# Attention output of a gated layer on one TensorE: rows from score weights instead of columns from value weights

## Chip, cores and metric

The kernel runs on one core of a Trainium2 chip. The metric is the device time of one execution in microseconds (us).

## What is computed

The layer has two parts. The first is a gated long convolution over heads (`_L0_xattn_ref`), the second a routed linear attention (`_L0_ffn_ref`). The change touches only the end of the second part. Cut to that, the reference is:

```python
qk = einsum('bhld,bhmd->bhlm', q_exp, k_exp) * HDK ** (-0.5)
qk = qk * tril(ones)                      # causal mask, no softmax
o = einsum('bhlm,bhmd->bhld', qk, v)      # 16 heads, v is 32 wide in each
mu, var = mean(o, -1), var(o, -1)         # of each head's 32 values
o = (o - mu) / sqrt(var + EPS)
out = (silu(g) * o.reshape(b, l, d)) @ Wout
x = x + tanh(g_ffn) * out
```

All of it is in float32. The mean over a head is taken out of `Wv` during setup, so `o` has mean zero and its variance is the mean of its squares.

## The kernel before

A step handles one slice of the batch and head axes: a tile of 128 rows by 512 columns. There are 32 slices (`NH`) and 35 steps, h from -2 to 32, written out one after another. A step works on four slices at different stages: `pre` makes the products and the normalised query of slice h+2 and h+3, `front` convolves slice h+1, `back` projects and scores slice h, and `tail` finishes slice h-1 (attention output, norm, gate, output projection). So the attention output runs in 32 steps, h = 1 to 32. In steps 31 and 32 there is no convolution left beside it.

Each engine has a program of its own, in an order fixed by hand, and the engines meet at semaphores. Nothing is planned at run time. What follows is the order on each engine around the change.

TensorE (L353 to L438): four transposes of z, convolutions 0 and 1 (`conv`, 3 and 6 matmuls of 512 columns), then `attention_output` (L325), then convolution 2 (9 matmuls), then four transposes of `oT` back into rows (L373), then `conv_last` (12 matmuls of 256 to 64 columns, L301), then the projections for q, k and the logits (L386 to L391, 24 matmuls), convolution 3, the count matmul (L398), the transposes of qn, the projection for v (L407), and further work, to the scores (L348) at the end of the step. `transpose4` is the helper of L265; the convolution matmuls carry L289, the projections L315.

`attention_output` (L325 to L335) waits for the four masks and for v. It makes 16 matmuls, one for each head. The stationary operand is a head's 32 columns of `v_sb`, the moving operand the head's 128 x 128 masked scores `att`. The output is 32 partitions by 128 columns, so four heads lie side by side in four column groups of the array. The result is the transpose of o. ScalarE copies it out of bank 4 into `oT` (L508), and TensorE transposes it back into bank 4 (L373).

ScalarE (L485 on): y_raw copies (L499), `kv_round` 0 (L483), copy of oT (L508), `kv_round` 1 (L483), the two Silu of y (L522, L524), Square of o (L529), then copies of q and k (L544, L547) and the query norm (L558, L562).

VectorE (L765 on): the multiply of convolution 0, y_conv (L773), the multiply of convolution 1, y low part (L784), statistics of x (L789 to L797), the multiply of convolution 2, the sum of squares (L803) and variance plus eps (L806), `multiply_last`, the router selection, then `gated` (L831, L836).

GpSimd (L641 on): products and low parts of kv 0 and 1 (L624 to L633), the power for the query norm (`rstd1`, L639 from L649), the power for the attention norm (`o_rstd`, L639 from L651), the rotation (L657 to L665), products 2 and 3, and the power for z.

SyncE issues all loads and stores of a step; the change does not touch it.

Of the kernel before, what the change touches and what calls it, by code (L numbers as in the profile page):

```python
# [13 lines left out]
P = 128  # L14
# [10 lines left out]
def can_wait(value):  # L25

    return not isinstance(value, int) or value > 0


def flamingo_gated_layer(nc, x, ctx_t, g_xattn, g_ffn, ssm_kernel, ssm_D, conv_w, Wq, Wk, Wv, Wg,  # L30
# [35 lines left out]
    with ExitStack() as stack:  # L66
        def sb(name, *free):
            return stack.enter_context(nc.sbuf_tensor(name, [P, *free], F32))
# [9 lines left out]
        def sem(name):  # L78
            return stack.enter_context(nc.semaphore(name))
# [65 lines left out]
        keT = sb("keT", CH, P)  # L145
        att = sb("att", CH, CH, P)
        o_sq = sb("o_sq", RH, HDV)
        oT = sb("oT", CH, P)
        gated = sb("gated", DV)
        out_sb = sb("out_sb", 2, L)  # L150
        yT_p = parts("yT", CH, P)
# [21 lines left out]
        gatedT_ps, zT_ps, out_ps, logit_ps, q_ps, v_ps, g_ps, cnt_ps = (  # L173
            sem(n) for n in ("gatedT_ps", "zT_ps", "out_ps", "logit_ps", "q_ps", "v_ps", "g_ps", "cnt_ps"))
        conv_ps = [sem(f"conv_ps{i}") for i in range(CH)]
        qeT_ps, keT_ps, qT_ps, xo_ps, oT_ps, o_ps = (
            sem(n) for n in ("qeT_ps", "keT_ps", "qT_ps", "xo_ps", "oT_ps", "o_ps"))
        attn_ps = [sem(f"attn_ps{i}") for i in range(CH)]

        gatedT_high, y_cur, y_ready, th_ready, qk_copied, v_copied, gate_ready = (  # L180
            sem(n) for n in ("gatedT_high", "y_cur", "y_ready", "th_ready", "qk_copied", "v_copied", "gate_ready"))
        qeT_sb, keT_sb, qx_ready, oT_sb, o_squared = (
            sem(n) for n in ("qeT_sb", "keT_sb", "qx_ready", "oT_sb", "o_squared"))
        y_high = sem("y_high")
        kv_high = [sem(f"kv_high{i}") for i in range(CH)]

# [75 lines left out]
        def _(eng):  # L262
            def transpose4(dst, src, last):
                for c in range(CH):
                    ins = nc.tensor.transpose(dst[:, c * P:(c + 1) * P], src(c), ident)  # L265
                ins.then_inc(last, 1)
# [55 lines left out]
            def step(t, p, q, tail, back, front, pre):  # L322
                h = 2 * t + p

                def attention_output():  # L325

                    for r in range(CH):
                        eng.wait_ge(mask_done[r], h)
                    eng.wait_ge(v_copied, h)
                    for c in range(CH):  # L330
                        for r in range(CH):
                            i = CH * c + r
                            ins = nc.tensor.matmul(bank[4][r * HDV:(r + 1) * HDV, c * P:(c + 1) * P],  # L333
                                                   v_sb[:, i * HDV:(i + 1) * HDV], att[:, r, c, :], start=True, stop=True)
                    ins.then_inc(oT_ps, 1)  # L335

                def scores():

# [29 lines left out]
                if front:  # L368
                    eng.wait_ge(mul_done[0], h + 2)
                    conv(p, 2, h + 1)  # L370
                if tail:
                    eng.wait_ge(oT_sb, h)
                    transpose4(bank[4], lambda c: oT[:, c, :], o_ps)  # L373
                if front:
                    if can_wait(h):
                        eng.wait_ge(mask_done[0], h)
# [66 lines left out]
        def _(eng):  # L443
# [41 lines left out]
            def step(t, p, q, tail, back, front, pre):  # L485
# [16 lines left out]
                if pre:  # L502
                    kv_round(p, 0, h + 2)
                if tail:
                    eng.wait_ge(oT_ps, h)
                    if can_wait(h - 1):
                        eng.wait_ge(o_ps, h - 1)
                    eng.activation(oT[:, :, :], bank[4][:, :].rearrange("p (c n) -> p c n", c=CH), ACT.Copy  # L508
                                   ).then_inc(oT_sb, 1)
                if pre:  # L510
                    kv_round(p, 1, h + 2)
                if first_step:
# [5 lines left out]
                if back:  # L518
# [3 lines left out]
                    eng.activation(yT_p[0][:, :, :], y_raw[:, :, :], ACT.Silu).then_inc(y_high, 1)  # L522
                    eng.wait_ge(y_high, h + 1)
                    eng.activation(y_raw[:, :, :], y_raw[:, :, :], ACT.Silu).then_inc(y_ready, 1)  # L524
                if tail:
                    eng.wait_ge(o_ps, h)
                    if can_wait(h - 1):
                        eng.wait_ge(o_summed, h - 1)
                    eng.activation(o_sq[:, :, :], bank[4][:, :].rearrange("p (a n) -> p a n", n=HDV), ACT.Square  # L529
                                   ).then_inc(o_squared, 1)  # L530
                if isinstance(h, int) and h == 0:
                    output_weights_high()
                if first_step:
# [35 lines left out]
                if back:  # L569
                    eng.wait_ge(v_ps, h + 1)  # L570
                    if can_wait(h):
                        eng.wait_ge(oT_ps, h)
                    eng.activation(v_sb[:, :], bank[4][:, :], ACT.Copy).then_inc(v_copied, 1)
                if tail:
                    eng.wait_ge(gatedT_ps, h)
# [33 lines left out]
        @block.gpsimd  # L609
        def _(eng):  # L610
            eng.memset(minus_half[:, :], -0.5).then_inc(half_ready, 1)
            eng.wait_ge(half_ready, 1)
            eng.wait_ge(s_consts, 16)

            def products(t, p, c, h2):

                if c == 0:
                    eng.wait_ge(s_kx[p], 16 * (t + 2))

                if c >= 2:  # L620
                    eng.wait_ge(kv_ready[c - 2], h2 + 1)
                elif can_wait(h2):
                    eng.wait_ge(kv_ready[c + 2], h2)
                eng.tensor_tensor(view(kv[:, c % 2, 0:FULL], [[ROW, NROT], [1, ROW]]),  # L624
                                  view(kx[:, p, c, 0:ROW], [[0, NROT], [1, ROW]]),
                                  view(kx[:, p, c, 0:ROW], [[NB, NROT], [1, ROW]]), ALU.mult)
                eng.tensor_tensor(kv[:, c % 2, FULL:FULL + HALF], kx[:, p, c, 0:HALF],  # L627
                                  kx[:, p, c, HALF:2 * HALF], ALU.mult).then_inc(kv_made[c], 1)

            def kv_rest(p, c, h2):  # L630

                eng.wait_ge(kv_high[c], h2 + 1)
                eng.tensor_tensor(kv_p[1][:, p, c, :], kv[:, c % 2, :], kv_p[0][:, p, c, :].bitcast(F32), ALU.subtract  # L633
                                  ).then_inc(kv_ready[c], 1)


            def rsqrt(dst, src, n, ready, value, done):
                eng.wait_ge(ready, value)
                eng.tensor_tensor(dst[:, 0:n], src[:, 0:n], minus_half[:, 0:n], ALU.pow).then_inc(done, 1)  # L639

            def step(t, p, q, tail, back, front, pre):  # L641
                h = 2 * t + p
                if pre:
                    products(t, p, 0, h + 2)
                    products(t, p, 1, h + 2)
                    kv_rest(p, 0, h + 2)
                    kv_rest(p, 1, h + 2)
                if pre:
                    rsqrt(rstd1, ve1, 1, ve1_ready, h + 3, rstd1_ready)  # L649
                if tail:  # L650
                    rsqrt(o_rstd, o_ve, RH, o_ve_ready, h, o_rstd_ready)  # L651
                if back:

                    eng.wait_ge(qk_copied, h + 1)
                    if can_wait(h):
                        eng.wait_ge(qke_ready, h)
                    eng.tensor_tensor(rot_a[:, :, :], qk_sb[:, :, :], view(const[:, C_COS:C_COS + 1], [[0, 2 * RH], [1, HDK]]),  # L657
                                      ALU.mult).then_inc(rot_prod, 1)
                    hf = HDK // 2
                    for a in range(2):  # L660
                        s = const[:, C_SIN + a * hf:C_SIN + a * hf + 1]
                        eng.tensor_tensor(rot_b[:, :, a * hf:(a + 1) * hf], qk_sb[:, :, (1 - a) * hf:(2 - a) * hf],  # L662
                                          view(s, [[0, 2 * RH], [1, hf]]), ALU.mult).then_inc(rot_prod, 1)
                    eng.wait_ge(rot_prod, 3 * h + 3)
                    eng.tensor_tensor(rot_a[:, :, :], rot_a[:, :, :], rot_b[:, :, :], ALU.add).then_inc(rot_ready, 1)  # L665
                if pre:
                    products(t, p, 2, h + 2)
                    products(t, p, 3, h + 2)
                    kv_rest(p, 2, h + 2)
                    kv_rest(p, 3, h + 2)  # L670
                if front:
                    rsqrt(rstd2, ve2, 1, ve2_ready, h + 2, rstd2_ready)

            run(eng, step)

        @block.vector
        def _(eng):
# [84 lines left out]
            def step(t, p, q, tail, back, front, pre):  # L762
# [12 lines left out]
                    ins.then_inc(y_conv, 1)  # L775
                if front:
                    multiply(p, 1, h + 1)
                if setup_step:
                    weights_low(1)
                if back:  # L780
# [16 lines left out]
                    eng.tensor_scalar(ve1[:, :], mv1[:, 1:2], EPS, None, ALU.add).then_inc(ve1_ready, 1)  # L797
                if front:
                    multiply(p, 2, h + 1)
                if tail:  # L800

                    eng.wait_ge(o_squared, h)
                    eng.tensor_reduce(o_var[:, :], o_sq[:, :, :], AX_X, ALU.add).then_inc(o_summed, 1)  # L803
                    eng.wait_ge(o_summed, h)
                    eng.wait_ge(eps_ready, h)
                    eng.scalar_tensor_tensor(out=o_ve[:, :], in0=o_var[:, :], scalar=1.0 / HDV, in1=eps_w[:, :],  # L806
                                             op0=ALU.mult, op1=ALU.add).then_inc(o_ve_ready, 1)
                if front:
                    multiply_last(p, h + 1)
                if back:  # L810
# [75 lines left out]
                if back:  # L886
                    for r in range(CH):
                        eng.wait_ge(attn_ps[r], h + 1)
                        if r == 0 and can_wait(h):
                            eng.wait_ge(oT_ps, h)  # L890
                        mask_scores(r)

            run(eng, step)
# [47 lines left out]
```

## Time and profile before

| what | value |
|---|---|
| median of 3 runs | 985.41 us (985.02 to 985.78) |
| profiled execution, its own time | 986.2 us |
| its span | 984.4 us |
| TensorE clock granted, mean | 0.982 of full |
| TensorE matmul busy | 923.5 us, 94% |
| TensorE weight load busy | 792.4 us, 81% |
| VectorE, GpSimd, ScalarE busy | 624.8, 673.0, 426.9 us |

Busy time of TensorE is modelled and matmuls overlap, so 94% does not say that every cycle is used. It says that nearly no time passes without a matmul under way. Weight loads (PEld) are listed apart and run beside the matmuls. A float32 matmul that is not a transpose shows as two records of PE and two of PEld, so 16 matmuls show as 32.

### The profile page before, as it was taken

What the parts mean: (1) busy time and instruction counts of PE and PEld (TensorE: products, weight loads), DVE (VectorE), ACT (ScalarE), POOL (GpSimd) and SP (SyncE); (2) the same over time, 40 slices, a digit from 0 to 9 for tenths busy, and PEclk for the clock granted to TensorE, in tenths of its full rate; (3) what the DMA queues carried; (4) which work ended last, traced back from release to release, by engine and by line L of the source; (5) the groups of instructions that cost most, each with busy time, mean ns of one, the idle gap of its engine ahead of it and who ended that gap; (6) DMA issues with size and microseconds to landing.
All of it is one profiled execution on the core that took longest, in us unless ns stands there. A gap on an engine that the chain in (4) does not pass through costs nothing.

```text
span 984.4 us, 18833 instructions
## 1 busy us (share of the span) xinstructions
PE 923.5 (94%) x7168; PEld 792.4 (81%) x7168; DVE 624.8 (63%) x1400; ACT 426.9 (43%) x906; POOL 673.0 (68%) x613
## 2 busy tenths in 40 slices
PE   1598999999999999999999999999999999999973
PEld 1487888888888888888888888888888888888862
DVE  4765666667666666766666676666666766666542
ACT  2464444444444444444444444444444444454320
POOL 6676668776666777766677776667777666686321
PEclk9899999999999999999999999999999999999996
DMA  8111221012222201222220122222112222210000
GB/s 278 50 46 47 60 60 49 17 55 60 61 59 60 57 21 43 60 61 60 60 60 21 39 60 61 59 61 59 36 28 58 60 61 60 60 41 11 5 11 21
DMA packets 25992, 52.50 MB, mean 53 GB/s; under 512 B 2544, under 2 KB 3696, under 8 KB 25904
## 3 DMA queue, kind: packets, MB, share of 16 engines
q1 hardware_dynamic: 22304, 46.59, 17.5%
q10 hardware_dynamic: 3600, 4.72, 1.5%
q8 instruction: 57, 0.93, 0.4%
q14 instruction: 31, 0.25, 0.1%
HBM read 42.75 MB, written 8.55 MB: 52 GB/s over the span
## 4 chain that ended last, share of the span: by engine, by line
PE 81%; DMA 5%; issue 5%; POOL 4%; DVE 3%; ACT 1%; SPq 0%; POOLq 0%; ACTq 0%
PE bank L315 33%; PE bank L289 19%; PE bank L276 11%; PE bank L265 8%; DMA x_in<-in_x 4%; PE bank L301 4%; PE bank L348 3%; PE bank L333 3%; POOL o_rstd L639 2%; DMA w_all<-in_L_ffn_Wv 1%; POOL rstd L639 1%; POOL rot_b L662 1%; POOL kv_low L633 0%; DVE gated L831 0%; DVE out_sb L884 0%
## 5 line engine op out<-in xcount | busy, mean ns | idle before, releaser
L633 POOL TENSOR_TENSOR kv_low<-kv,kv_high 128x576 fp32r<-128x576 f32 x128 | 182.1, 1435 | 136.8 <-ACT kv_high L483 136.8
L289 PE MATMUL bank<-kv_high,toep 128*128 128x512 f32 x640 | 225.2, 409 | 11.0 <-DVE z_terms L736 5.6
L624 POOL TENSOR_TENSOR kv<-kx 128x512 f32<-128x512 f32 x128 | 159.5, 1246 | 6.6 <-DMA const<-shape_consts 6.6
L289 PEld LDWEIGHTS bank<-kv_high,toep 128*128 128x128 f32 x640 | 122.5, 191 | 42.3 <-DVE z_terms L736 11.5
L639 POOL TENSOR_TENSOR o_rstd<-o_ve,minus_half 128x16 f32<-128x16 f32 x32 | 93.1, 2910 | 79.8 <-DVE o_ve L806 79.8
L289 PE MATMUL bank<-kv_low,toep 128*128 128x512 f32 x320 | 126.8, 396 | 0.0
L483 ACT ACTIVATE kv_high<-kv 128x576 fp32r<-128x576 f32 x128 | 87.7, 688 | 87.6 <-POOL kv L627 87.6
L315 PE MATMUL bank<-w_all_high,yT_high 128*128 128x512 f32 (+2 forms) x512 | 119.7, 355 | 3.0 <-DVE gated L831 3.0
L276 PE MATMUL bank<-const,z_terms 128*128 128x128 f32 x1024 | 117.1, 273 | 1.0 <-ACT qx L472 1.0
L276 PEld LDWEIGHTS bank<-const,z_terms 128*128 128x128 f32 x1024 | 112.8, 140 | 1.3 <-ACT qx L472 1.2
L315 PE MATMUL bank<-w_all_low,yT_high 128*128 128x512 f32 (+2 forms) x512 | 112.5, 341 | 0.0
L315 PE MATMUL bank<-w_all_high,yT_low 128*128 128x512 f32 (+2 forms) x512 | 106.7, 341 | 0.0
L884 DVE TENSOR_TENSOR out_sb<-bank,x 128x512 f32<-128x512 f32 x32 | 22.1, 692 | 125.6 <-PE bank L315 125.6
L746 DVE TENSOR_TENSOR qke<-rot_a,sel 128x1024 f32<-128x1024 f32 x32 | 69.1, 2160 | 38.9 <-POOL rot_a L665 38.9
L315 PEld LDWEIGHTS bank<-w_all_low,yT_high 128*128 128x128 f32 x512 | 83.8, 189 | 11.2
L741 DVE TENSOR_TENSOR att<-bank,const 128x512 f32<-128x512 f32 x128 | 79.5, 683 | 18.6 <-PE bank L348 18.6
L315 PEld LDWEIGHTS bank<-w_all_high,yT_low 128*128 128x128 f32 x512 | 81.6, 189 | 11.7
L732 DVE TENSOR_TENSOR z_terms<-bank,qx 128x512 f32<-128x512 f32 x128 | 85.3, 667 | 4.2 <-PE bank L289 4.1
L315 PEld LDWEIGHTS bank<-w_all_high,yT_high 128*128 128x128 f32 x512 | 78.4, 189 | 10.1 <-DVE gated L831 4.3
L639 POOL TENSOR_TENSOR rstd<-ve,minus_half 128x1 f32<-128x1 f32 x64 | 36.7, 573 | 69.1 <-DVE ve L797 60.1
L627 POOL TENSOR_TENSOR kv<-kx 128x64 f32<-128x64 f32 x128 | 73.3, 573 | 0.0
L736 DVE TENSOR_TENSOR z_terms<-bank,qx 128x384 f32<-128x384 f32 x128 | 69.8, 545 | 0.0
(101 smaller groups left out, 1621.6 us busy)
## 6 DMA issues: line engine op xcount, KB each, us to landing
toep<-taps_dram SPq DMA_DIRECT2D x32, 512.0 KB, 7.1
kx<-in_ctx SPq DMA_DIRECT2D x32, 384.0 KB, 7.4
x_in<-in_x SPq DMA_DIRECT2D x32, 256.0 KB
out_x<-out_sb SPq DMA_DIRECT2D x32, 256.0 KB
w_all<-in_L_ffn_Wv ACTq DMA_DIRECT2D x1, 1024.0 KB, 12.6
w_all<-in_L_ffn_Wg ACTq DMA_DIRECT2D x1, 1024.0 KB, 11.0
w_out<-in_L_ffn_Wout ACTq DMA_DIRECT2D x1, 1024.0 KB, 17.1
router<-in_L_ffn_router_w ACTq DMA_DIRECT2D x1, 512.0 KB, 7.1
```

The lines of the kernel that those rows point to most:

```text
L265: ins = nc.tensor.transpose(dst[:, c * P:(c + 1) * P], src(c), ident)
L276: ins = nc.tensor.matmul(bank[2][:, c * P:(c + 1) * P], z_terms[:, c, i * ROW:(i + 1) * ROW], ident, is_transpose=True, start=(c == 0 and ...
L289: ins = nc.tensor.matmul(bank[lc % 2][:, :], toep[:, 1 - p, a, (lc - mc) * P:(lc - mc + 1) * P], kv_p[b][:, 1 - p, mc, 0:FULL], start=(mc ...
L315: ins = nc.tensor.matmul(dst[:, 0:cols], src_p[a][:, c, :], w_p[b][:, c, c0:c0 + cols], start=(i == 0 and c == 0), stop=(i == len(PASSES) ...
L483: eng.activation(kv_p[0][:, p, c, :], kv[:, c % 2, :], ACT.Copy).then_inc(kv_high[c], 1)
L624: eng.tensor_tensor(view(kv[:, c % 2, 0:FULL], [[ROW, NROT], [1, ROW]]), view(kx[:, p, c, 0:ROW], [[0, NROT], [1, ROW]]), view(kx[:, p, c, ...
L627: eng.tensor_tensor(kv[:, c % 2, FULL:FULL + HALF], kx[:, p, c, 0:HALF], kx[:, p, c, HALF:2 * HALF], ALU.mult).then_inc(kv_made[c], 1)
L633: eng.tensor_tensor(kv_p[1][:, p, c, :], kv[:, c % 2, :], kv_p[0][:, p, c, :].bitcast(F32), ALU.subtract).then_inc(kv_ready[c], 1)
L639: eng.tensor_tensor(dst[:, 0:n], src[:, 0:n], minus_half[:, 0:n], ALU.pow).then_inc(done, 1)
L732: eng.tensor_tensor(view(z_terms[:, lc, 0:1], [[ROW, NROT], [1, ROW]]), view(y[:, 0:1], [[ROW, NROT], [1, ROW]]), view(q, [[NB, NROT], [1, ...
L736: eng.tensor_tensor(view(z_terms[:, lc, first:first + 1], [[ROW + NB, NROT - 1], [1, ROW]]), view(y[:, ROW:ROW + 1], [[ROW, NROT - 1], [1, ...
L741: eng.tensor_tensor(att[:, r, :, :], bank[SCORE_BANKS[r]][:, :].rearrange("p (c n) -> p c n", c=CH), view(mask[:, 0:1], [[0, CH], [1, P]]) ...
```

## The change

The attention output swaps its operands. The masked scores become the stationary operand (128 x 128) and a head's 32 columns of v the moving one. The output is 128 rows by 32 columns for each head, already in rows. The transposes back, the copy into `oT` and the tile itself go. Square on ScalarE takes the place of the copy. The sum of squares and the variance move up on VectorE, ahead of y low, and the attention norm's power on GpSimd moves ahead of that of the query norm.

```diff
 # TensorE, attention_output
-                            i = CH * c + r
-                            ins = nc.tensor.matmul(bank[4][r * HDV:(r + 1) * HDV, c * P:(c + 1) * P],
-                                                   v_sb[:, i * HDV:(i + 1) * HDV], att[:, r, c, :], start=True, stop=True)
-                    ins.then_inc(oT_ps, 1)
+                            cols = slice((CH * c + r) * HDV, (CH * c + r + 1) * HDV)
+                            ins = nc.tensor.matmul(bank[4][:, cols], att[:, r, c, :], v_sb[:, cols], start=True, stop=True)
+                    ins.then_inc(o_ps, 1)
...
-                if tail:
-                    eng.wait_ge(oT_sb, h)
-                    transpose4(bank[4], lambda c: oT[:, c, :], o_ps)
...
 # ScalarE, between kv_round 0 and kv_round 1
-                    eng.wait_ge(oT_ps, h)
+                    eng.wait_ge(o_ps, h)
                     if can_wait(h - 1):
-                        eng.wait_ge(o_ps, h - 1)
-                    eng.activation(oT[:, :, :], bank[4][:, :].rearrange("p (c n) -> p c n", c=CH), ACT.Copy
-                                   ).then_inc(oT_sb, 1)
+                        eng.wait_ge(o_summed, h - 1)
+                    eng.activation(o_sq[:, :, :], bank[4][:, :].rearrange("p (a n) -> p a n", n=HDV), ACT.Square
+                                   ).then_inc(o_squared, 1)
...
 # ScalarE, after the two Silu of y
-                if tail:
-                    eng.wait_ge(o_ps, h)
-                    if can_wait(h - 1):
-                        eng.wait_ge(o_summed, h - 1)
-                    eng.activation(o_sq[:, :, :], bank[4][:, :].rearrange("p (a n) -> p a n", n=HDV), ACT.Square
-                                   ).then_inc(o_squared, 1)
...
 # GpSimd
+                if tail:
+                    rsqrt(o_rstd, o_ve, RH, o_ve_ready, h, o_rstd_ready)
                 if pre:
                     rsqrt(rstd1, ve1, 1, ve1_ready, h + 3, rstd1_ready)
-                if tail:
-                    rsqrt(o_rstd, o_ve, RH, o_ve_ready, h, o_rstd_ready)
...
 # VectorE: this block stands behind multiply(p, 1) now, and stood behind multiply(p, 2)
                 if tail:
                     eng.wait_ge(o_squared, h)
                     eng.tensor_reduce(o_var[:, :], o_sq[:, :, :], AX_X, ALU.add).then_inc(o_summed, 1)
                     eng.wait_ge(o_summed, h)
                     eng.wait_ge(eps_ready, h)
                     eng.scalar_tensor_tensor(out=o_ve[:, :], in0=o_var[:, :], scalar=1.0 / HDV, in1=eps_w[:, :],
                                              op0=ALU.mult, op1=ALU.add).then_inc(o_ve_ready, 1)
```

The waits for `oT_ps` elsewhere (the copy of v on ScalarE, the masks on VectorE) become waits for `o_ps`.

## Rows read from the trace of the kernel before

**Rows 1.** The page: busy time and count of TensorE, and its clock by slice.
```profile
PE 923.5 (94%) x7168; PEld 792.4 (81%) x7168; DVE 624.8 (63%) x1400; ACT 426.9 (43%) x906; POOL 673.0 (68%) x613
...
PEclk9899999999999999999999999999999999999996
```

**Rows 2.** The critical chain through one middle step: start, length, what.
```profile
508.59 0.59 PE bank L265 x4
...
511.35 1.08 PE bank L333 x32
...
514.70 0.44 PE bank L265 x4
...
516.42 2.98 PE bank L315 x24
...
536.98 0.59 PE bank L265 x4
```

**Rows 3.** Timeline at the end of `conv_last`: start, length. 515.66 and 516.22: five loads apart.
```profile
515.66 0.19 PEld L301 LDWEIGHTS bank<-kv_low,toep 128*128 128x128 f32 x1
...
516.03 0.28 PE L301 MATMUL bank<-kv_low,toep 128*128 128x64 f32 x1
...
516.22 0.54 PEld L315 LDWEIGHTS bank<-w_all_high,yT_high 128*128 128x128 f32 x4
```

**Rows 4.** Weight loads at the count matmul and behind it, in order of time.
```profile
521.98 0.19 PEld L398 LDWEIGHTS bank<-u,const 128*128 128x128 f32 x1
522.00 0.22 PEld L265 LDWEIGHTS bank<-const,qn 128*128 128x128 f32 x1
```

**Rows 5.** Groups by form: weight loads, count, busy us, mean ns of one.
```profile
L333 PEld LDWEIGHTS bank<-att,v_sb 128*32 128x32 f32 x1024 | 27.6, 111 | 20.3 <-issue 20.3
...
L265 PEld LDWEIGHTS bank<-const,oT 128*128 128x128 f32 x128 | 16.0, 141 | 6.1 <-ACT oT L508 2.1
...
L398 PEld LDWEIGHTS bank<-u,const 128*128 128x128 f32 x64 | 11.9, 188 | 3.6 <-DVE u L819 1.2
```

**Rows 6.** Timeline of the same step on ScalarE, GpSimd and VectorE.
```profile
512.48 0.60 ACT L508 ACTIVATE oT<-bank 128x512 f32<-128x512 f32 x1 [1.55 <-PE bank L333]
...
512.98 0.68 ACT L483 ACTIVATE kv_high<-kv 128x576 fp32r<-128x576 f32 x1
...
513.55 0.62 ACT L522 ACTIVATE yT_high<-y_raw 128x512 fp32r<-128x512 f32 x1
...
513.73 1.43 POOL L633 TENSOR_TENSOR kv_low<-kv,kv_high 128x576 fp32r<-128x576 f32 x1 [1.30 <-ACT kv_high L483]
...
515.17 0.60 ACT L529 ACTIVATE o_sq<-bank 128x512 f32<-128x512 f32 x1 [0.33 <-PE bank L265]
...
516.86 0.55 POOL L639 TENSOR_TENSOR rstd<-ve,minus_half 128x1 f32<-128x1 f32 x1 [1.70 <-DVE ve L797]
...
517.76 0.67 DVE L803 TENSOR_REDUCE o_var<-o_sq 128x16 f32<-128x512 f32 x1
...
518.73 2.91 POOL L639 TENSOR_TENSOR o_rstd<-o_ve,minus_half 128x16 f32<-128x16 f32 x1 [1.31 <-DVE o_ve L806]
```

**Rows 7.** Waits over the whole span: total us, times, longest.
```profile
PE bank L315 <- DVE gated L831: 3.0, 6, 1.5
```

**Rows 8.** Stretches: PE, PEld, DVE, ACT, POOL busy, then granted clock, DMA.
```profile
525.50:529.50 4.00, 4.00 (x38) 3.98 (x37) 2.23 (x2) 1.77 (x3) 4.00 (x4) 1.00 0.01 2
...
944.00:948.00 4.00, 1.60 (x9) 1.19 (x8) 2.15 (x6) 0.94 (x5) 4.00 (x3) 1.00 0.00 0
948.00:951.00 3.00, 3.00 (x9) 2.33 (x8) 0.85 (x4) 0.00 (x0) 2.48 (x3) 0.50 0.02 5
```

**Rows 9.** Timeline of the last step, and durations of line 301's loads (min/median/max).
```profile
962.28 1.94 PE L333 MATMUL bank<-att,v_sb 128*32 128x128 f32 x32 [2.76 <-DVE att L741]
...
966.07 0.60 ACT L529 ACTIVATE o_sq<-bank 128x512 f32<-128x512 f32 x1 [1.21 <-PE bank L265]
```
```profile
L301 PEld LDWEIGHTS bank<-kv_high,toep x256: 187/192/329, 35.6 to 915.3; 128*128 128x128 f32 x128
```

More of the change, by code:

```diff
@@ L147, in flamingo_gated_layer @@
         o_sq = sb("o_sq", RH, HDV)
-        oT = sb("oT", CH, P)
         gated = sb("gated", DV)
@@ L175, in flamingo_gated_layer @@
         conv_ps = [sem(f"conv_ps{i}") for i in range(CH)]
-        qeT_ps, keT_ps, qT_ps, xo_ps, oT_ps, o_ps = (
-            sem(n) for n in ("qeT_ps", "keT_ps", "qT_ps", "xo_ps", "oT_ps", "o_ps"))
+        qeT_ps, keT_ps, qT_ps, xo_ps, o_ps = (sem(n) for n in ("qeT_ps", "keT_ps", "qT_ps", "xo_ps", "o_ps"))
         attn_ps = [sem(f"attn_ps{i}") for i in range(CH)]
@@ L181, in flamingo_gated_layer @@
             sem(n) for n in ("gatedT_high", "y_cur", "y_ready", "th_ready", "qk_copied", "v_copied", "gate_ready"))
-        qeT_sb, keT_sb, qx_ready, oT_sb, o_squared = (
-            sem(n) for n in ("qeT_sb", "keT_sb", "qx_ready", "oT_sb", "o_squared"))
+        qeT_sb, keT_sb, qx_ready, o_squared = (sem(n) for n in ("qeT_sb", "keT_sb", "qx_ready", "o_squared"))
         y_high = sem("y_high")
@@ L571, in step @@
                     if can_wait(h):
-                        eng.wait_ge(oT_ps, h)
+                        eng.wait_ge(o_ps, h)
                     eng.activation(v_sb[:, :], bank[4][:, :], ACT.Copy).then_inc(v_copied, 1)
@@ L777, in step @@
                     multiply(p, 1, h + 1)
+                if tail:
+                    eng.wait_ge(o_squared, h)
+                    eng.tensor_reduce(o_var[:, :], o_sq[:, :, :], AX_X, ALU.add).then_inc(o_summed, 1)
+                    eng.wait_ge(o_summed, h)
+                    eng.wait_ge(eps_ready, h)
+                    eng.scalar_tensor_tensor(out=o_ve[:, :], in0=o_var[:, :], scalar=1.0 / HDV, in1=eps_w[:, :],
+                                             op0=ALU.mult, op1=ALU.add).then_inc(o_ve_ready, 1)
                 if setup_step:
@@ L799, in step @@
                     multiply(p, 2, h + 1)
[L800 to L807, printed above, removed]
                 if front:
@@ L889, in step @@
                         if r == 0 and can_wait(h):
-                            eng.wait_ge(oT_ps, h)
+                            eng.wait_ge(o_ps, h)
                         mask_scores(r)
```

## The prediction

> **What bounds the kernel now.** I read the page first. TensorE shows a matmul under way for 94% of the span, and VectorE, GpSimd and ScalarE are at 63, 68 and 43% [rows 1]. A busy share is only an average, so the chain of waits through one middle step came next. From one step's first transposes at 508.59 to the next one's at 536.98 is 28.39 us, and the chain stays on TensorE throughout [rows 2]. So in the middle of the run a step costs what TensorE's program costs, and the change is worth what it adds to and takes from that program, unless it makes another engine late. Third, the forms and single records of weight loads, since the change turns a 32-column load into a 128-column one. Last, the timeline of ScalarE and GpSimd for what is moved, and the windows for the clock.
>
> The attention output is in 32 steps: 1024 records, 32 in each [rows 5]. Thirty of them (h = 1 to 30) have convolution beside them and are like the one shown. The last two are emptier and are priced apart.
>
> **What it removes on TensorE.** In the chain, `attention_output` takes 1.08 us for its 32 records [rows 2], which is 0.034 us each. That is possible only because four heads sit in four column groups and go side by side. This stretch is replaced. The four transposes back take 0.44 us [rows 2] and go.
>
> **What it adds on TensorE.** There are again 16 float32 matmuls, thus 32 records, but each now loads 128 columns of weights over the whole array and streams only 32 columns of v past them. No row shows just that form. Two neighbours bound it from both sides. The upper one is a load of 128 columns with few moving columns, line 301: from 515.66 to 516.22 five loads go by, 0.112 us each, while the moving operand shrinks from 128 to 64 columns [rows 3]. Fewer moving columns do not bring them closer; so the load sets the pace, and with 32 columns it should too. The lower one is today's 0.034 us per record. The operands of line 301 are the rounded kind of float32, those of the new matmuls plain float32. For plain float32 there is the count matmul: its loads last 188 ns, like the 192 of line 301, against 111 for today's 32-column loads and 141 for transposes [rows 5, 9]. Behind the count matmul's second load the next one starts 0.02 us later but lasts 0.22 instead of 0.14, so it was held up by 0.08 us: the load ahead of it kept the path for about 0.10 [rows 4, 5]. That is nearest to the upper neighbour, and I take 0.112. Then 32 loads are 3.57 us, and with the 0.07 us of run-out that the old 1.08 us also holds, 3.64 us.
>
> The Trainium skill (TensorE: Matmul & The Clock Gate, LDWEIGHTS) says that a load takes its number of columns divided by 1.2, in ns, whatever the rows. By that 128 columns are an estimated 107 ns, the new stretch would be 0.15 us shorter, and the sum 5 us lower. The trace agrees in kind (111 against 188 ns for 32 and 128 columns) and shows 112 as the pace, which the sum uses.
>
> Per middle step: 3.64 - 1.08 - 0.44 = **+2.12 us**, and thirty steps give +63.6 us.
>
> **What it moves.** On ScalarE a copy of 0.60 us is dropped and Square, also 0.60, takes its place [rows 6]. Square starts when the new stretch ends: 511.35 + 3.64 = 514.99. Behind it in the queue stand `kv_round` 1 (0.68) and the Silu that makes y high (0.62) [rows 6], so y high is ready at about 515.05 + 0.60 + 0.68 + 0.62 = 516.95 at the earliest, with the gaps between operations 517.0. TensorE needs it at 516.42 today and at 516.42 + 2.12 = 518.54 then [rows 2]: 1.6 us to spare. The second Silu and y low come some 1.4 us later (an operation of about that size on each engine), and the first matmul that reads y low stands behind sixteen others of 2.98 / 24 = 0.124 us [rows 2]. This does not cost anything; without that slack the cost would be what exceeds 1.6 us. `kv_round` 1 moves from 512.98 to 515.65, and GpSimd's low part behind it (1.43 us) ends at some 517.8. The norm's sum on VectorE (0.67 us) and the short variance come by some 516.7, before that. VectorE's own queue has nothing late in it: what the sum is moved ahead of (y low, the statistics) waits for the Silus until 517.6 anyway. The attention power of 2.91 us [rows 6] then runs from 517.8 to 520.7; before it ended at 521.64, in a step that is 2.12 us shorter. The query norm's power (0.55 us) now stands behind it and ends near 521.3. Its reader on ScalarE is queued behind the copies of q and k, which end only when the projections do (516.42 + 2.98 + 2.12 = 521.52 or later) [rows 2]. So this too is hidden by the longer program. No DMA is moved and no transfer issued differently; SP's queue sees nothing.
>
> One wait is relieved: `gated` on VectorE, which the v projection waited for, is ready some 3 us earlier relative to TensorE. That wait cost PE 3.0 us over the run [rows 7]. I take **-3.0**; its bounds are 0 and -3.0.
>
> **The last two steps.** In step 31 TensorE waits for the norm, so the path is what counts: 3.64 - 1.08 (attention) - 0.60 (copy) - about 0.60 (transposes with their run-out, as in rows 2) = **+1.4**, bounds 0 and 2.1. In step 32 attention to Square takes 966.07 - 962.28 = 3.79 us, at the low clock of 1.2 GHz (half) [rows 9]. The new stretch is then 32 loads. At the low clock loads of line 301 reach 329 ns instead of 192 [rows 9], 0.137 more, which would make 0.25 us each if all of it held the next one up; if the pace simply doubles, 0.22. With 0.22: 7.1 + 0.3 = 7.4 us, so +3.6; I take **+3.5**, with 0 as the lower end (loads not slowed) and 4.6 as the upper.
>
> **Sum.** 63.6 - 3.0 + 1.4 + 3.5 = +65.5 us. The profiled execution took 986.2 us (span 984.4 and 1.8 around it), so the changed kernel would take 1051.7; the median of the runs shown is 0.8 below the profiled one, hence **1051 us**. A measurement of this kernel can tell about 0.2% (2 us) from no change.
>
> **The rivals.**
>
> *Loads as cheap as today (faster).* The place is the 32 records in `attention_output`. If a full-array load were hidden behind the one before it and each record cost 0.026 us, as might be read from the 0.02 us between the load of line 398 and the next [rows 4], the new stretch would be 0.83 + 0.07 = 0.90 us, the step 0.90 - 1.08 - 0.44 = -0.62 and the run -18.6 - 3.0 - 1 = some -23 us: 963. It decides from 0.045 us per record downward, where 32 records cost less than the 1.52 us removed. Against it stand the five loads in 0.56 us at few moving columns and the prolonged load [rows 3, 4]. The Trainium skill (TensorEngine Tiling (Array Packing), Instruction Overhead) gives about 60 cycles for each matmul however few its columns, an estimated 25 ns at 2.4 GHz. By that alone the change would win; the trace agrees with it nowhere that 128 columns of weights are loaded. The same page (When to Use Tiling) advises, for a moving operand of 32 columns, to swap the operands and tile by columns, the opposite of this change. Chance 0.05, and 0.01 that it ends between the two within 0.2%.
>
> *Only one of the two loads of a float32 matmul costs full price (slower, half as much).* The pair at line 398 could be read as 0.026 + 0.112 = 0.138 us. Then 16 pairs take 2.2 + 0.07 us, a step +0.76, the run +23 - 3 + 2: 1007. Against: both loads last 188 ns, and the hold-up of 0.08 us [rows 4, 5]. Chance 0.07.
>
> *The clock falls in each step (much slower).* During 3.6 us the array would stream 32 columns per 0.112 us, so it does little although the records say busy. The trace shows a fall to 1.2 GHz after 944 to 948 with PE busy for 1.60 of 4 us [rows 8]. If it fell in each step and stayed low for about 3 us as in 948 to 951, some 1.5 us more per step, 45 in all: 1096. Against it: 525.5 to 529.5 is all transposes, which load and stream little beyond that, and the clock stays at 1.00; and in the middle it never falls [rows 1, 8]. Chance 0.07.
>
> **How the numbers follow.** The load mechanism with 0.112 us has 0.80. Its own range: at 0.105 us per load a step is 0.22 us cheaper, -6.7; the last step may cost nothing, -3.5; together 1041. Upward: a few unseen tenths per step (a late Silu or a late qn, 0.3 us, +9) and 1 us in the last step: 1061. The other cases hold 0.20, so the range is that of the likeliest, 1041 to 1061. Slower is 0.80 + 0.07 + 0.07 = 0.94, faster 0.05, same 0.01.
>
> **What would show it.** In the changed profile: line 333's successor with PEld records of about 188 ns, 0.11 apart, and a chain piece of about 3.6 us in place of 1.08; no transposes of oT; a step of 30.5 us in place of 28.4; convolution 2 starting right behind attention; `gated` off the list of TensorE's waits; a granted clock of 1.0 throughout the middle. The forecast is wrong if the records are closer than 0.1 us, if the clock dips in each step, or if TensorE shows a new idle time in front of the projections (y high late) or of the transposes of qn (query norm late).

## The result, and the profile after

The changed kernel takes 1089.12 us (median of four, 1081.91 to 1096.78) against 985.5 us. That is slower by a factor of 1.106 (95% interval 1.102 to 1.109). The range was 1041 to 1061, so the direction was right and the size was not: 66 us more were forecast and 104 more measured. The profiled execution was the shortest of the four; it took 1081.9 us and its span is 1080.1 us. The forecast made for a profiled execution was 1051.7.

The page of the changed kernel: busy time, and the clock granted to TensorE in 40 slices, as in [rows 1].

```profile
PE 1021.0 (95%) x7040; PEld 895.5 (83%) x7040; DVE 673.7 (62%) x1400; ACT 404.0 (37%) x874; POOL 684.7 (63%) x613
...
PEclk9799999999989999998899998899999988999986
```

TensorE's busy share is as before (95% against 94%). But the clock, which stood at 9 all through the middle in [rows 1], now shows eights in groups (9 is 90% or more of the full clock, 8 is 80 to 90%). That is the first thing to see. The second is in the chain of waits through two middle steps. The first of them has no fall of the clock (compare [rows 2]):

```profile
202.54 2.08 PE bank L286 x9
204.62 0.09 issue
204.71 3.73 PE bank L330 x32
208.44 2.15 PE bank L286 x9
210.59 1.28 PE bank L298 x12
211.87 2.98 PE bank L312 x24
...
235.21 3.73 PE bank L330 x32
```

and the second has one:

```profile
485.20 2.08 PE bank L286 x9
487.29 0.09 issue
487.38 4.57 PE bank L330 x32
491.94 4.00 PE bank L286 x9
495.94 1.77 PE bank L298 x12
497.71 3.01 PE bank L312 x24
...
521.26 4.34 PE bank L330 x32
```

Line 330 is the attention output (line 333 before), line 286 a convolution, 298 `conv_last`, 312 the projections. In the first step the sum of the forecast holds nearly to the digit: the attention takes 3.73 us in the chain (3.64 were forecast), the transposes are gone, and from 204.71 to 235.21 is 30.50 us, where 28.39 + 2.12 = 30.51 had been worked out. In the second the attention, convolution 2 and `conv_last` together take 10.34 instead of 7.16 us, and the step is 33.88. In a step without a fall the records of single matmuls start 0.111 to 0.112 us apart, and the first matmul of convolution 2 follows 3.565 us after the first of the attention; 32 x 0.112 was 3.57.

The windows of the second step, and the next one, say why (PE, PEld, DVE, ACT, POOL busy, then the granted clock):

```profile
487.38:490.00 2.62, 2.62 (x24) 2.62 (x24) 2.62 (x8) 0.00 (x0) 1.06 (x1) 1.00 1.01 281
490.00:496.80 6.80, 6.80 (x25) 5.93 (x24) 4.32 (x10) 2.32 (x4) 3.46 (x2) 0.50 0.31 92
521.26:524.20 2.94, 2.94 (x27) 2.94 (x27) 2.71 (x8) 0.00 (x0) 0.91 (x1) 1.00 0.94 273
524.20:531.00 6.80, 6.80 (x25) 5.93 (x25) 4.62 (x10) 2.32 (x4) 4.00 (x2) 0.50 0.26 81
```

PE is busy for all of each window, and PEld for all of the two that lie ahead of a fall. Yet the clock falls to 1.2 GHz (0.50 of full) 2.7 us after the attention output has begun, and is low for 6.8 us, through the rest of it and the convolution behind it. The DMA share (next to last number) is near 1 ahead of the falls, but it is 0.96 in the same stretch of wide128 below, where the clock does not fall, so busy DMA queues alone do not make it fall.

Over the whole trace there are 12 such falls in the middle (from the first to the thirtieth attention), eight of 6.8 us and four of 3.4, 68.3 us together. Every one begins between 2.47 and 3.39 us after an attention output has begun. In the kernel before there is none between 81 and 948 us.

Thus the account of the profiled execution, against the kernel before: from the first to the thirtieth attention output the 29 middle steps take 917.35 us against 827.82, which is 89.5 more. Without a fall they would take 30.494 each (the median of the 17 that have none) against a mean of 28.546, which is 56.5 us. The falls add 33.0. What lies behind the start of the thirtieth attention has grown by 6.4 us. The forecast had 29 x 2.12 - 3.0 = 58.5 for the first, 2.1 + 1.4 + 3.5 = 7.0 for the last, and nothing for the falls.

In the second trace of the changed kernel (after_again below, an execution of 1089.2 us and so near the median) there are 15 falls, 85.3 us together, and by the same working they add 924.68 - 29 x 30.500 = 40.2 us. So the falls account for the excess of the median as well.

### The profile page after: what moved, and what is told of

Read it like the earlier page. It is cut to its first block, busy times and chain, and to the rows that moved or that the text cites. A ratio compares the mean times of both kernels' runs of the same rounds, so it can differ in the third digit from the quotient of the medians.

```text
span 1080.1 us, 18514 instructions
## 1 busy us (share of the span) xinstructions
PE 1021.0 (95%) x7040; PEld 895.5 (83%) x7040; DVE 673.7 (62%) x1400; ACT 404.0 (37%) x874; POOL 684.7 (63%) x613
## 4 chain that ended last, share of the span: by engine, by line
PE 91%; issue 3%; POOL 2%; DVE 2%; DMA 1%; ACT 1%; POOLq 0%; ACTq 0%
PE bank L312 33%; PE bank L286 22%; PE bank L330 11%; PE bank L273 10%; PE bank L262 7%; PE bank L298 4%; PE bank L344 3%; DMA w_all<-in_L_ffn_Wv 1%; POOL rot_b L649 0%; POOL kv_low L620 0%; PE bank L391 0%; DVE w_all L695 0%; POOLq L66 0%; POOL rstd L626 0%; POOL rot_a L652 0%
## 5 line engine op out<-in xcount | busy, mean ns | idle before, releaser
L286 PE MATMUL bank<-kv_high,toep 128*128 128x512 f32 x640 | 239.6, 433 | 11.2 <-DVE z_terms L723 6.0
L286 PEld LDWEIGHTS bank<-kv_high,toep 128*128 128x128 f32 x640 | 132.8, 208 | 39.1 <-DVE z_terms L723 6.4
L330 PEld LDWEIGHTS bank<-v_sb,att 128*128 128x128 f32 x1024 | 127.4, 206 | 21.1 <-issue 21.1
L330 PE MATMUL bank<-v_sb,att 128*128 128x32 f32 x1024 | 130.3, 289 | 8.6 <-DVE att L728 5.0
L626 POOL TENSOR_TENSOR o_rstd<-o_ve,minus_half 128x16 f32<-128x16 f32 x32 | 104.1, 3254 | 48.5 <-DVE o_ve L771 45.3
L286 PE MATMUL bank<-kv_low,toep 128*128 128x512 f32 x320 | 134.7, 421 | 0.0
L719 DVE TENSOR_TENSOR z_terms<-bank,qx 128x512 f32<-128x512 f32 x128 | 87.6, 685 | 13.0 <-PE bank L286 13.0
L846 DVE SCALAR_TENSOR_TENSOR x<-bank,gates,x_in 128x512 f32<-128x512 f32 x32 | 24.0, 751 | 91.1 <-PE bank L273 91.1
L501 ACT ACTIVATE o_sq<-bank 128x512 f32<-128x512 f32 x32 | 19.1, 598 | 152.5 <-PE bank L330 152.5
```

The lines of the kernel that those rows point to most:

```text
L286: ins = nc.tensor.matmul(bank[lc % 2][:, :], toep[:, 1 - p, a, (lc - mc) * P:(lc - mc + 1) * P], kv_p[b][:, 1 - p, mc, 0:FULL], start=(mc ...
L330: ins = nc.tensor.matmul(bank[4][:, cols], att[:, r, c, :], v_sb[:, cols], start=True, stop=True)
L719: eng.tensor_tensor(view(z_terms[:, lc, 0:1], [[ROW, NROT], [1, ROW]]), view(y[:, 0:1], [[ROW, NROT], [1, ROW]]), view(q, [[NB, NROT], [1, ...
```

## Theories

Theory **C, the clock:** the excess is TensorE at 1.2 GHz. The cause is that the attention output now loads weights without a pause and streams only 32 columns for each load. Rival **L:** a long row of full-array loads lowers the clock whatever is streamed. Rival **M:** the new order of the norm, or the missing transposes, does it. For the runs that price small terms the rivals are named with the runs.

## Experiments

### Stream more columns for each load (wide128, wide64)

```diff
-                            cols = slice((CH * c + r) * HDV, (CH * c + r + 1) * HDV)
+                            cols = slice((CH * c + r) * HDV, min((CH * c + r) * HDV + 128, DV))
```

A head's weights also meet the v columns of its three right-hand neighbours (the last three heads have fewer neighbours and stream 96, 64 and 32 columns). Those results land where the next heads write their own, so the output stays the same. wide64 has 64 in place of 128.

> The changed kernel, but each of the 32 records of the attention output streams 128 columns of v past its weights instead of 32 (what lies beyond the head's own 32 columns is overwritten by the next heads, so the output stays the same). The number and size of the weight loads stay. Theory C (the excess over the forecast, 1081.9 profiled against 1051.7, is TensorE at 1.2 GHz in 12 of 30 middle steps, because the stretch streams only 32 columns per load): the loads keep their pace of 0.112 us, the stretch stays at 3.6 us, the granted clock is 1.00 in all middle steps, and the time is 1046 to 1056 us. Rival L (a long row of full-array loads lowers the clock whatever is streamed): falls as before, 1080 to 1097. Rival M (the moved norm or the missing transposes lower it): the same 1080 to 1097.

Measured: 1047.58 us (1046.02 to 1048.0). The chain and the window of the same stretch in wide128:

```profile
509.79 3.73 PE bank L330 x32
513.52 2.17 PE bank L286 x9
515.68 1.28 PE bank L298 x12
```
```profile
509.79:513.40 3.61, 3.61 (x33) 3.61 (x33) 2.87 (x8) 0.00 (x0) 1.06 (x1) 1.00 0.96 272
```

Up to four times the columns cost nothing: the stretch is 3.73 us as before, so the load sets the pace and not what is streamed. The clock does not fall once in the middle steps, here or in two more traces with 128 columns (wide128_again and wide128_old_order below), and 41.5 us are back. The loads are the same in number and size as in the changed kernel, so rival L falls; the norm has the new order and the transposes are absent, so rival M falls too. What is left of the change at the full clock is still a loss: 62 us against the kernel before.

> As wide128, but with 64 columns of v streamed for each load, twice the changed kernel's 32 and half of wide128's. Theory C (too little is streamed per load): the loads keep their pace, and if twice the columns are enough the middle steps stay at 2.4 GHz and the time is 1046 to 1052 us; if not, falls remain in some steps and the time is between 1055 and 1095. Rival L (the loads alone decide, already contradicted by wide128): as the changed kernel.

Measured: 1051.18 us (1050.55 to 1052.99), again without a fall in the middle. So in this stretch 64 columns for each load keep the clock as 128 do. The few us between the two lie behind the start of the thirtieth attention (83.3 us of the span in wide64, 78.2 in wide128), where the clock falls in both kernels.

### The order of the norm put back (undo_moves)

Square, variance and attention power stand where they stood before; the matmuls stay as changed.

```diff
-                if tail:
-                    rsqrt(o_rstd, o_ve, RH, o_ve_ready, h, o_rstd_ready)
                 if pre:
                     rsqrt(rstd1, ve1, 1, ve1_ready, h + 3, rstd1_ready)
+                if tail:
+                    rsqrt(o_rstd, o_ve, RH, o_ve_ready, h, o_rstd_ready)
...
```

> The changed kernel with Square, the variance and the attention power put back where they stood in the kernel before; the matmuls stay as changed, the transposes and the copy stay away. Theory C: the same falls of the clock in about 12 middle steps, 1080 to 1097 us, and at most 3 us for the order of the norm. Rival M (it is the new order): no falls, 1046 to 1058.

Measured: 1091.56 us (1080.04 to 1094.37), with 15 falls in the middle and a median of 30.505 us for the steps without one. The falls are there with either order of the norm.

### The stretch cut in two (split_halves)

The norm stands in its old order, as in undo_moves, and eight of the 16 matmuls move behind convolution 2.

```diff
                 if tail:
-                    attention_output()
+                    attention_output(0)
                 if front:
                     eng.wait_ge(mul_done[0], h + 2)
                     conv(p, 2, h + 1)
+                if tail:
+                    attention_output(1)
```

> As undo_moves, but the 16 matmuls of the attention output are cut in two: eight ahead of convolution 2, eight behind it, so that a stretch with little streamed lasts 1.8 us instead of 3.6 with 2.1 us of 512-column matmuls between. Theory C: no falls in the middle steps, 1048 to 1058 us. Rival L with the sum over a step deciding and not the length of one stretch: falls remain, 1080 to 1097.

Measured: 1050.30 us (1049.08 to 1051.04). The chain and a window over both halves:

```profile
509.59 1.95 PE bank L330 x16
511.54 2.16 PE bank L286 x9
513.70 1.70 PE bank L330 x16
```
```profile
509.59:515.40 5.81, 5.81 (x42) 5.42 (x43) 4.94 (x15) 1.42 (x3) 2.65 (x3) 1.00 0.79 234
```

The same loads with the same 32 columns, 1.8 us at a time with 2.2 us of 512-column matmuls between, keep the clock at 1.00. What a whole step streams is the same as in undo_moves, and the falls are gone (none in the middle): it matters what is done in one piece. The time is inside the 1048 to 1058 that theory C gave.

### A shorter and a longer stretch (heads12, twice)

heads12 leaves out every fourth head, so a quarter of the attention output is not computed. twice makes the 16 matmuls two times over, writing the same values again. The first edit is that of heads12.

```diff
-                        for r in range(CH):
+                        for r in range(CH - 1):
```
```diff
-                    for c in range(CH):
+                    for c in [c for _ in range(2) for c in range(CH)]:
```

> The changed kernel with every fourth head of the attention output left out: 24 records instead of 32, and a stretch of 24 x 0.112 = 2.7 us. In the changed kernel the clock fell 2.5 to 3.4 us after the stretch began. Theory C with the length of the stretch: no or hardly a fall, and 1048 - 30 x 0.89 = 1021 us (1014 to 1030). If it is only the share of streaming over a whole step: falls in some steps and 1035 to 1065. For the price of a load: the middle steps without a fall are 0.89 us shorter than the changed kernel's 30.49.

Measured: 1052.82 us (1047.83 to 1054.42). That is outside the 1014 to 1030 that I had given for a shorter stretch, and inside the 1035 to 1065 of its rival, by which the share of streaming over a whole step decides. The rival is not the account all the same: split_halves streams as little over a step as undo_moves and has no fall. Two of its steps in the chain, the first with a fall and the second without:

```profile
511.74 2.84 PE bank L330 x24
514.58 3.72 PE bank L286 x9
518.30 1.28 PE bank L298 x12
...
542.95 2.84 PE bank L330 x24
545.79 2.16 PE bank L286 x9
547.95 1.28 PE bank L298 x12
```

The load's price is as forecast: the steps without a fall take 29.608 us, 0.886 less than 30.494 for eight loads fewer, 0.111 each. But my reading of the length was wrong. With a stretch of 2.7 us the clock still falls in 19 of the 29 steps, for 3.4 us each time. It falls 2.5 to 3.4 us after the stretch has begun, when the stretch is over or nearly over, so the convolution behind it pays (3.72 us instead of 2.16). Of the lengths that ran, only the 1.8 us of split_halves were without a fall.

> The changed kernel with the 16 matmuls of the attention output made twice (the same values written again): 64 records, a stretch of 7.14 us. By the loads alone the run is 30 x 3.57 = 107 us longer than at a full clock, and some 10 in the last two steps: 1165 us. Theory C: the clock falls in every middle step, since no position of the stretch escapes any more; the second part of the stretch and the convolution behind it then run at half pace, about 3.3 to 5 us more per step: 1250 to 1320 us. Rival (the falls come by chance of neighbours and not by the stretch): falls in some steps only, 1190 to 1210.

Measured: 1310.29 us (1309.09 to 1312.55). Chain and window of one step:

```profile
509.29 10.72 PE bank L330 x64
520.01 3.58 PE bank L286 x9
...
548.26 8.92 PE bank L330 x64
```
```profile
509.29:520.00 10.71, 10.71 (x65) 10.71 (x66) 2.87 (x8) 0.00 (x0) 1.07 (x1) 0.66 0.46 129
```

All 29 middle steps now have a fall, where the changed kernel has 12. The 64 loads would take 7.1 us at the full clock and take 8.3 to 11.3. The time is inside the 1250 to 1320 of theory C, and the rival's 1190 to 1210 is far off.

### The changed kernel again (after_again)

> The changed kernel once more, on the chip that runs these experiments. Theory C: which steps see the fall depends on where in time the stretch comes, so the spread between executions stays large (1080 to 1097 us) while the steps without a fall take 30.5 us each.

Measured: 1089.85 us (1087.86 to 1091.55), ratio 1.107 (1.105 to 1.108). Its profiled execution has 15 falls of the clock in the middle instead of 12, in other steps, and 14 steps without one, at a median of 30.500 us. The spread of these four was smaller than I said; over all eight executions it is 1081.9 to 1096.8, against 983.5 to 988.0 for all runs of the kernel before.

### The norm's order alone (norm_up_only, wide128_old_order)

norm_up_only is the kernel before with the attention power ahead of the query norm's and the variance right behind y low (in the change it stands ahead of y low). Square on ScalarE stays where it was. The part on VectorE begins:

```diff
                     eng.tensor_tensor(yT_p[1][:, :, :], y_raw[:, :, :], yT_p[0][:, :, :].bitcast(F32), ALU.subtract
                                       ).then_inc(y_low, 1)
+                if tail:
+                    eng.wait_ge(o_squared, h)
+                    eng.tensor_reduce(o_var[:, :], o_sq[:, :, :], AX_X, ALU.add).then_inc(o_summed, 1)
...
```

> The kernel before, with only the second half of the change: the variance behind y low on VectorE instead of behind the multiply of convolution 2, the attention power ahead of the query norm's on GpSimd. Matmuls, copy and transposes stay as before. If my term holds (TensorE waits 3.0 us for gated in six steps, and the move removes it) the time is 982 to 983.5 us, 0.2 to 0.35% faster, and the line 'PE ... <- DVE gated' leaves the waits. Rival: the wait moves to another place (y low late, query norm late) and the time stays at 985 to 986.

Measured: 982.71 us (981.01 to 983.92, ten executions), ratio 0.9970 (0.9961 to 0.9979). An eleventh execution took 5196 us; why is not known, and it is left out. This beats both kernels, by a margin that is small but clear of noise. The first wait of norm_up_only shown here answers to [rows 7]. The second is VectorE's own wait for the attention power, which was 48.4 us in 31 times before:

```profile
PE bank L315 <- DVE gated L831: 0.2, 1, 0.2
```
```profile
DVE gated L831 <- POOL o_rstd L639: 3.0, 1, 3.0
```

TensorE's wait goes from 3.0 us to 0.2, and the time follows: 2.5 us less by the medians (985.17 to 982.71), 3.0 by the ratio, 2.8 by the wait.

The change's own order of the norm (wide128_again) and the old one (wide128_old_order) in the longer program, with the clock steady:

> wide128 once more, as the partner of the next run on the same chip: 1046 to 1049 us, no fall of the clock in the middle steps.

> wide128 with Square, variance and attention power at their places of the kernel before, so that the order of the norm is priced in the longer program with the clock steady (in undo_moves against the changed kernel the falls hide it). My term of 3.0 us for the order: 1050 to 1051. Its rival, from the trace of undo_moves, where TensorE waits only 0.2 us for gated although the order is the old one (the relief comes from the longer or steadier program and not from the order): the same as wide128 within 1 us.

Measured: 1047.55 us (1046.74 to 1048.78) and 1045.80 (1045.60 to 1049.17), ratios 1.0631 (1.0612 to 1.065) and 1.0623 (1.0602 to 1.0644), which cannot be told apart. The 1050 to 1051 that my term gave for the old order did not come. In the longer program the new order brings nothing that these runs can see. TensorE's wait for `gated` is 0.2 us with the new order and 1.0 with the old one, both in a single step, where the kernel before had 3.0. And the new order has a price of its own in step 31: Square now stands ahead of the Silu that makes y high, and with no convolution between them TensorE waits for y high. The changed kernel shows it, wide128_again has the same 1.20 us, and there is no such wait in wide128_old_order or in the kernel before:

```profile
1035.74 1.22 PE L312 MATMUL bank<-w_all_high,yT_high 128*128 128x256 f32 x4 [1.20 <-ACT yT_high L515]
```

So the longer program takes away most of the wait for `gated` by itself, and the order of the norm could have gained some 3 us in the kernel before, without the new matmuls.

## Why the prediction was wrong

**The term that failed** is the clock. The prediction expected "a granted clock of 1.0 throughout the middle", and its sum has nothing for a fall; the third rival, "The clock falls in each step", had a chance of 0.07, and its price stood outside the range. The runs showed falls in the middle that cost 33.0 us in one profiled execution and 40.2 in the other.

Two things were wrong with how the rival was weighed. First, the evidence against: "525.5 to 529.5 is all transposes, which load and stream little beyond that, and the clock stays at 1.00" [rows 8]. A transpose streams 128 columns for each load, just what wide128 does, and wide128 keeps the clock. That stretch was the wrong neighbour for 32 columns for each load. The prediction itself said that no row shows just that form, and so the price of a fall should have been in the range.

Second, the case was drawn as all or nothing. The clock fell in 12 and 15 of the 29 steps of two profiled executions, and the cost of the low stretches was 33.0 / 68.3 = 0.48 us for each us at 1.2 GHz. The rival had priced 1.5 us for each step; a step with a fall cost 33.0 / 12 = 2.75, but not every step had one. With the 33.0 the sum comes to 1051.7 + 33.0, less 2.0 in the middle steps and 0.6 in the last, which is 1082.1 against 1081.9 profiled. These terms are read from that same trace, so this is bookkeeping; the proof that the clock is the missing term is wide128, which takes it away and lands inside the range.

**The load's price** was right: 0.112 us, 3.57 for 32, from a neighbour of another number format and from one prolonged load. The trace after has 3.565, heads12 0.111 by difference, and wide128 the same with four times the columns. The stationary operand sets the pace, and so two of the rivals are gone (loads as cheap as today, and half the pair for free). The Trainium skill (TensorE: Matmul & The Clock Gate, LDWEIGHTS) gives an estimated 107 ns for 128 columns. That lies 4% under the pace measured at the full clock, 0.1115 us. At the low clock the measured pace is 0.213 us, twice the estimate. Whether the pace goes with the number of columns no run tests, since every new load has 128.

**The step** was right: 28.39 + 2.12 = 30.51 us forecast, 30.49 to 30.51 us measured as the median of the steps at the full clock. wide128, the changed kernel but for the clock, takes 1047.6 us, inside the range.

**What moved in the queues** cost nothing in the middle steps, as forecast. Here are ScalarE, VectorE and TensorE of the step that begins its attention at 204.71:

```profile
208.48 0.60 ACT L501 ACTIVATE o_sq<-bank 128x512 f32<-128x512 f32 x1 [4.18 <-PE bank L330]
...
209.55 0.62 ACT L515 ACTIVATE yT_high<-y_raw 128x512 fp32r<-128x512 f32 x1
...
211.71 0.72 PE L312 MATMUL bank<-w_all_high,yT_high 128*128 128x256 f32 x4
```

y high is ready at 210.17 and read at 211.71: 1.54 us to spare, where 1.6 had been worked out. Step 31 is the exception, with the 1.20 us of waiting for y high shown above. The prediction named only the norm as what TensorE waits for in that step.

**The relieved wait**, -3.0 us, is there in the trace (3.0 to 0.2 us), but the reason given for it was only a part. With the old order the longer program already brings it to 1.0 us (wide128_old_order) or 0.2 (undo_moves).

**The last two steps.** In step 32 attention to Square was 1062.43 - 1056.00 = 6.43 us instead of 3.79, so +2.6 where +3.5 was taken. The loads slow down with the clock, from 0.112 to 0.213 us; the 0.22 of the prediction was near, but the first loads of the stretch still ran at the full clock.

```profile
1056.00 6.40 PE L330 MATMUL bank<-v_sb,att 128*128 128x32 f32 x32 [2.79 <-DVE att L728]
...
1062.43 0.60 ACT L501 ACTIVATE o_sq<-bank 128x512 f32<-128x512 f32 x1 [12.34 <-PE bank L330]
```

**What stays open.** It is not shown which of the middle steps see a fall. That differs between executions of one kernel, but there is a pattern. In both traces of the changed kernel the falls come in groups of three steps in a row (steps 7 to 9, 14 to 16, 19 to 21 and 26 to 28 of the first trace). Within a group each fall begins further behind the begin of its stretch than the one before it, for instance 2.49, 2.92 and 3.35 us, and the third is the one that lasts 3.4 us instead of 6.8. This fits a fall that hangs on where in time the stretch lies, but no run fixed that place. Lengths and columns between those that ran were not tried.

## What to carry to other kernels

Before swapping operands, price the weight load: with 128 columns of weights and few columns to stream, the load was the whole cost here (0.112 us each, with 32 columns or with 128), and four column groups side by side can be worth more than a transpose back. Then look at how long TensorE would go on streaming little in one piece: a busy PE row does not show it, but the granted clock does. Cutting the stretch in two, with 2.2 us of 512-column matmuls between, or streaming useless columns, which was free under a load, kept the full clock here. Where no stretch of the kernel resembles the new one, the clock belongs in the range.

## What the runs showed that I had not expected

- The clock fell with TensorE busy throughout by the profile (PE 2.62 of 2.62 us, PEld too, in front of the fall shown at 490).
- More work made it faster: 128 columns for each load instead of 32 took 1047.6 us instead of 1089.1.
- A VectorE operation on 16 columns, the variance plus eps, takes a mean of 1243 ns in the changed kernel against 175 before and in undo_moves. The group of it after:

```profile
L771 DVE SCALAR_TENSOR_TENSOR o_ve<-o_var,eps_w 128x16 f32<-128x16 f32 x32 | 39.8, 1243 | 1.1
```

In 29 of the 32 steps it comes at its new place while GpSimd makes its low part of kv, and ends with it. In the last three steps GpSimd makes none and the operation, at the same place in VectorE's queue, takes 0.17 us. One step of each kind:

```profile
526.89 1.42 POOL L620 TENSOR_TENSOR kv_low<-kv,kv_high 128x576 fp32r<-128x576 f32 x1 [4.72 <-ACT kv_high L476]
526.99 1.35 DVE L771 SCALAR_TENSOR_TENSOR o_ve<-o_var,eps_w 128x16 f32<-128x16 f32 x1
...
1005.06 0.17 DVE L771 SCALAR_TENSOR_TENSOR o_ve<-o_var,eps_w 128x16 f32<-128x16 f32 x1
```

So it goes with what GpSimd does at the same time, and not with the place in the queue; what in the two operations makes one wait for the other, no run shows. It is off the path here: the power that waits for it stands behind the same GpSimd operation anyway.
